# Expert weights loaded by column parts, and exp taken straight from the score PSUM, in a gated cross-attention block with a mixture of experts

## What is computed

```python
# x (8, 100, 512), ctx (8, 722, 512), mask (8, 722) bool, H = 512, one head of D = 32
n = layernorm(x)
q, k, v = n @ Wq + bq, ctx @ Wk + bk, ctx @ Wv + bv
s = q @ k.T / sqrt(512)
s = (s - mean(s)) / (std(s, ddof=1) + 1e-8)            # over the 722 keys
attn = softmax(s + where(mask, -1e-32, 0))
x = x + tanh(g_xattn) * (tile(attn @ v, 16) @ Wout + bout)
n = layernorm(x)
w, idx = top2(softmax(n @ router_w.T)); w = w / (w.sum() + 1e-6)
# 8 experts, w13 (8, 512, 2048), w2 (8, 1024, 512)
y = sum over the two experts of w * ((silu(n @ gate) * (n @ up)) @ w2)
x = x + tanh(g_ffn) * y
```

## Time and profile before

| | us |
|---|---|
| median of 3 runs | 531.41 |
| lowest, highest | 523.58, 532.26 |
| profiled execution, its own time | 529.5 |
| its span in the trace | 527.9 |
| mean granted clock of TensorE in it | 0.858 |

### The profile page before, as it was taken

One profiled execution on the slowest core, in us unless ns is written; L12 is line 12 of the kernel. 1 busy time (PEld: TensorE's weight loads), 2 busy tenths in 40 slices (PEclk: granted clock), 3 DMA queues, 4 the chain that ended last, 5 costly groups with the idle time before them and its releaser, 6 DMA issues.

```text
span 527.9 us, 7587 instructions
## 1 busy us (share of the span) xinstructions
PE 422.1 (80%) x2108; PEld 307.7 (58%) x2109; DVE 243.1 (46%) x491; ACT 195.6 (37%) x319; POOL 194.9 (37%) x340
## 2 busy tenths in 40 slices
PE   3668986888662129999994099999999999999991
PEld 1234554445441127778773078777877877787781
DVE  0245663445545131475571454138537557367220
ACT  0032331232424211473560552237447266265220
POOL 2433475676657421234343003220413434235121
PEclk9796895766755559999998579999999999999997
DMA  7554665449210007626816706901492671880021
GB/s 220 174 185 159 192 201 130 151 152 353 76 34 13 0 21 264 236 40 199 321 34 230 279 0 214 333 23 23 130 368 42 222 291 30 285 265 21 5 40 13
DMA packets 25795, 78.78 MB, mean 149 GB/s; under 512 B 6041, under 2 KB 6049, under 8 KB 20658
## 3 DMA queue, kind: packets, MB, share of 16 engines
q1 hardware_dynamic: 19266, 67.51, 35.4%
q0 software_dynamic: 4752, 7.80, 8.2%
q10 hardware_dynamic: 1760, 3.28, 2.0%
HBM read 71.92 MB, written 7.57 MB: 151 GB/s over the span
## 4 chain that ended last, share of the span: by engine, by line
PE 61%; POOL 11%; DMA 9%; issue 8%; DVE 4%; SPq 2%; ACT 1%; POOLq 1%; DVEq 0%; ACTq 0%
PE scp L476 16%; PE turnA L456 16%; PE turnB L456 15%; PE kvp L463 2%; PE kvp L410 2%; DMA stage<-in_L_ffn_w_dram 2%; PE kvp L332 2%; POOL lists_d L969 2%; DMA ent_next<-lists_d 2%; DMA xg<-xn_d,gidx 2%; PE scp L442 1%; PE turnA L425 1%; POOL hot L998 1%; DMA g_in<-in_g_ffn_dram 1%; POOL rs L921 1%
## 5 line engine op out<-in xcount | busy, mean ns | idle before, releaser
L691 DVE TENSOR_TENSOR w13l<-stage,w13h 128x1024 fp32r<-128x1024 f32 x64 | 76.4, 1219 | 26.2 <-ACT w13h L537 25.8
L537 ACT ACTIVATE w13h<-stage 128x1024 fp32r<-128x1024 f32 x64 | 64.7, 1052 | 22.5 <-DMA stage<-in_L_ffn_w_dram 22.5
L476 PE MATMUL scp<-w2h,hTh 128*128 128x512 f32 x128 | 56.8, 444 | 2.3 <-DVE hTl L862 2.3
L456 PE MATMUL turnA<-w13h,xTh 128*128 128x512 f32 x128 | 53.2, 416 | 4.8 <-DVE xTl L851 4.8
L456 PE MATMUL turnB<-w13h,xTh 128*128 128x512 f32 x128 | 51.9, 406 | 0.0
L476 PE MATMUL scp<-w2l,hTh 128*128 128x512 f32 x128 | 51.6, 403 | 0.0
L456 PE MATMUL turnA<-w13l,xTh 128*128 128x512 f32 x128 | 51.5, 403 | 0.0
L456 PE MATMUL turnA<-w13h,xTl 128*128 128x512 f32 x128 | 51.5, 403 | 0.0
L476 PE MATMUL scp<-w2h,hTl 128*128 128x512 f32 x128 | 51.2, 400 | 0.0
L456 PE MATMUL turnB<-w13h,xTl 128*128 128x512 f32 x128 | 50.6, 395 | 0.0
L456 PE MATMUL turnB<-w13l,xTh 128*128 128x512 f32 x128 | 50.5, 395 | 0.0
(11 more groups left out here) (167 smaller groups left out, 737.2 us busy)
## 6 DMA issues: line engine op xcount, KB each, us to landing
stage<-in_L_ffn_w_dram SPq DMA_DIRECT2D x48, 1024.0 KB, 11.8
ctx_t<-in_ctx_dram SPq DMA_DIRECT2D x8, 1444.0 KB, 7.3
mterm<-mterm_d SPq DMA_DIRECT2D x8, 282.0 KB
x_t<-in_x_dram SPq DMA_DIRECT2D x8, 200.0 KB
out_dram<-x ACTq DMA_DIRECT2D x8, 200.0 KB
xn_d<-xn ACTq DMA_DIRECT2D x8, 200.0 KB
ctx_t<-in_L_xattn_Wout_dram SPq DMA_DIRECT2D x1, 1024.0 KB, 7.1
ent_next<-lists_d POOLq DMA_DIRECT2D x17, 1.0 KB, 2.0
```

What stands on the lines that cost most here:

```text
L456: mm = pe.matmul(region, xp[:, c, :], rhs, start=(c == 0 and i == 0), stop=(c == HC - 1 and i == 2))
L476: mm = pe.matmul(scp[:, 512:512 + H], hp[:, q, j * P:(j + 1) * P], wp[:, q * QC + j, :], start=(q == 0 and j == 0 and i == 0), stop=(q == ...
L537: act.activation(dst, src, ACT.Copy).then_inc(S["w_hi"], 1)
L691: dve.tensor_tensor(lo, raw, hi.bitcast(F32), ALU.subtract).then_inc(S["w_lo"], 1)
```

## The change

Expert weights: the host lays w13 out by column part (8 experts, 4 parts, 128 partitions, 2048 values: one part is 1 MB with 8 KB in a row for each partition) and w2 by halves in the same way. `stage13`, `w13h` and `w13l` have the part as their outer dimension. Part q is loaded when units 2q and 2q + 1 of the expert before are split; there is no wait for a gather except for the first. ACT waits for one part before the two units that read it.

Attention: exp is taken from `scp` in PSUM with scale and bias in one instruction, without z, maximum and accumulated sum. The mask becomes a factor `emask` = exp(term), 128 x 8 x 6, multiplied into the values when these are copied to `vn`. A 65th column of `vn` holds `emask` itself, so that the head has a 65th row with the softmax's sum. The bias row of the output is a 65th row of `wsum`: multiplied by the sum and divided again by it, it comes in with the output. The sum is brought to the partitions of the tokens by a matmul with one column (`pick_sum`), and its reciprocal is taken from there. x is kept in four buffers, so that `xc` is not needed.

```diff
-        mterm_d = nc.dram_tensor("mterm_d", [NB, SK], F32).ap()
-        stage13 = sb(es, "stage13", [P, HC, I2])
+        stage13 = sb(es, "stage13", [P, NQ, HC, 2 * QW])
-        x_t = [sb(a, f"x_t{i}", [SQ, H]) for i in range(2)]
+        x_t = [sb(a, f"x_t{i}", [SQ, H]) for i in range(4)]
-        vn = [sb(a, f"vn{i}", [P, KT, 2 * D]) for i in range(2)]
+        vn = [sb(a, f"vn{i}", [P, KT, 2 * D + 1]) for i in range(2)]
...
             for b in range(1, NB):
-                s = S[f"x_in{b % 2}"]
-                if b >= 2:
-                    sp.wait_ge(S["xn_ready"], b - 1)
-                    sp.wait_ge(S["xc_ready"], b - 1)
-                sp.dma_start(x_t[b % 2][:], x[b]).then_inc(s, 16)
-                load_mterm(b - 1)
+                if b >= 4:
+                    sp.wait_ge(S["x2_ready"], b - 3)
+                elif b == 2:
+                    sp.wait_ge(S["crow_done"], 1)
+                elif b == 3:
+                    sp.wait_ge(S["rw_turned"], 1)
+                sp.dma_start(x_t[b % 4][:], x[b]).then_inc(S[f"x_in{b % 4}"], 16)
...
             sp.wait_ge(S["attn_done"], 4)
+            sp.wait_ge(S["gathered"], 16)
             with sp.Fori(1, E) as e:
-                sp.wait_ge(S["w_lo"], e * W_UNITS - 2)
-                before = sp.value_load(first_tile[0:1, bass.ds(e - 1, 1)], min_val=0, max_val=TILES - 1)
-                sp.wait_ge(S["gathered"], before * 16 + 32)
-                for c in range(HC):
-                    sp.dma_start(stage13[:, c, :], w13[bass.ds(e, 1), c * P:(c + 1) * P, :].rearrange("o p n -> p (o n)")
-                                 ).then_inc(S[f"st13_{c}"], 16)
+                for q in range(NQ):
+                    sp.wait_ge(S["w_lo"], e * W_UNITS - W_UNITS + 2 * q + 2)
+                    sp.dma_start(stage13[:, q, :, :], w13[bass.ds(e, 1), q].rearrange("o p (c n) -> p (o c) n", c=HC)
+                                 ).then_inc(S[f"st13_{q}"], 16)
...
-            def softmax_z(b):
+            def softmax_exp(b):
                 act.wait_ge(S["sig_ready"], b + 1)
                 act.wait_ge(S["scores_done"], b + 1)
                 if b >= 1:
-                    act.wait_ge(S["exp_done"], b)
-                act.activation(z[:], scp[0:SQ, 0:SK], ACT.Identity, bias=sig[:, 5:6], scale=sig[:, 3:4]).then_inc(S["z_done"], 1)
-
-            def softmax_exp(b):
-                act.wait_ge(S["negmax"], b + 1)
-                if b >= 1:
                     act.wait_ge(S["prob_turned"], b)
-                    act.wait_ge(S["gsum"], b)
-                act.activation(prob[:], z[:], ACT.Exp, bias=zmax[:, 1:2], accum_out=psum_p[:]).then_inc(S["exp_done"], 1)
+                act.activation(prob[:], scp[0:SQ, 0:SK], ACT.Exp, bias=sig[:, 5:6], scale=sig[:, 3:4]).then_inc(S["exp_done"], 1)
 
             def split_hi(e, unit, last):
 
-                if unit == 0:
-                    for c in range(HC):
-                        act.wait_ge(S[f"st13_{c}"], e * 16 + 16)
+                if unit < 2 * NQ and unit % 2 == 0:
+                    act.wait_ge(S[f"st13_{unit // 2}"], e * 16 + 16)
...
                     pe.wait_ge(S["head_copied"], b + 1)
+                    if b == 0:
+                        pe.wait_ge(S["pick_made"], 2)
+                    pe.matmul(turnB[0:SQ, 640:641], headT[:], pick_sum[:], start=True, stop=True).then_inc(S["sum_done"], 1)
                     if live(i):
                         pe.wait_ge(S["v_copied"], 2 * (i + 1))
                     pe.matmul(turnA[0:SQ, 0:H], headT[:], wsum[:], start=True, stop=True).then_inc(S["out_done"], 1)
...
-                    dve.tensor_copy(vn[i % 2][:, 0:KT - 1, :], turnA[:, 0:(KT - 1) * 2 * D].rearrange("p (k d) -> p k d", d=2 * D)
-                                    ).then_inc(S["v_copied"], 1)
+                    dve.tensor_tensor(vn[i % 2][:, 0:KT - 1, 0:2 * D],
+                                      turnA[:, 0:(KT - 1) * 2 * D].rearrange("p (k d) -> p k d", d=2 * D),
+                                      emask[:, i, 0:KT - 1].unsqueeze(2).to_broadcast([P, KT - 1, 2 * D]), ALU.mult
+                                      ).then_inc(S["v_copied"], 1)
...
+                    dve.wait_ge(S["sum_done"], b + 1)
+                    if b >= 1:
+                        dve.wait_ge(S["x2_ready"], b)
+                    else:
+                        dve.wait_ge(S["tanh_done"], 1)
+                    dve.reciprocal(gs[:, 0:1], turnB[0:SQ, 640:641]).then_inc(S["sum_inv"], 1)
+                    dve.wait_ge(S["sum_inv"], b + 1)
+                    dve.tensor_scalar(gs[:, 1:2], gs[:, 0:1], g_t[0:SQ, 0:1], None, ALU.mult).then_inc(S["gsum"], 1)
                     dve.wait_ge(S["out_done"], b + 1)
...
             for i in ROUNDS:
+                if live(i):
+                    if i == 0:
+                        pool.wait_ge(S["emask_made"], 1)
+                    if i >= 2:
+                        pool.wait_ge(S["head_done"], i - 1)
+                    pool.tensor_copy(vn[i % 2][:, :, 2 * D:2 * D + 1], emask[:, i, :].unsqueeze(2)).then_inc(S["vsum_set"], 1)
...
-                if live(i + 1) and i >= 0:
-                    residual(i + 1)
```

More of the change, by code:

```diff
@@ L26, in gated_block @@
     D = Wq.shape[1]
-    E, _, I2 = w13.shape
-    I = I2 // 2
+    E, NQ, _, UW = w13.shape
     HC = H // P
+    QW = UW // HC // 2
+    I = NQ * QW
     IC = I // P
@@ L92, in gated_block @@
         qT = sb(a, "qT", [2 * D, SQ])
-        headT = sb(a, "headT", [2 * D, SQ])
-        xc = [sb(a, f"xc{i}", [SQ, H]) for i in range(3)]
+        headT = sb(a, "headT", [2 * D + 1, SQ])
+        pick_sum = sb(a, "pick_sum", [2 * D + 1, 1])
         x2 = [sb(a, f"x2{i}", [SQ, H]) for i in range(2)]
@@ L110, in gated_block @@
         g_t = sb(a, "g_t", [P, 2])
-        crow = sb(a, "crow", [SQ, H])
         tri = sb(a, "tri", [SQ, SQ])
@@ L319, in _ @@
             pe.wait_ge(S["wsum_copied"], 1)
-            pe.wait_ge(S["bv_spread"], 1)
             pe.wait_ge(S["small_in"], 16 * 7)
-            pe.matmul(scp[0:SQ, 0:H], bv_b[:], wsum[0:D, :], start=True, stop=False)
-            pe.matmul(scp[0:SQ, 0:H], ones[0:1, 0:SQ], bout_r, start=False, stop=True).then_inc(S["crow_done"], 1)
+            pe.matmul(scp[2 * D:2 * D + 1, 0:H], bv_c[:], wsum[0:D, :], start=True, stop=False)
+            pe.matmul(scp[2 * D:2 * D + 1, 0:H], ones[0:1, 0:1], bout_r, start=False, stop=True).then_inc(S["crow_done"], 1)
             pe.wait_ge(S["rw_copied"], 1)
@@ L407, in _ @@
                     pe.wait_ge(S["v_copied"], 2 * (b + 1))
+                    pe.wait_ge(S["vsum_set"], b + 1)
                     for k in range(KT):
                         n = P if k < KT - 1 else KL
-                        mm = pe.matmul(kvp[0:2 * D, 0:SQ], vn[b % 2][0:n, k, :], probT[0:n, k, :], start=(k == 0), stop=(k == KT - 1))
+                        mm = pe.matmul(kvp[0:2 * D + 1, 0:SQ], vn[b % 2][0:n, k, :], probT[0:n, k, :], start=(k == 0), stop=(k == KT - 1))
                     mm.then_inc(S["head_done"], 1)
@@ L454, in gate_up @@
                     for i, (xp, wp) in enumerate(terms):
-                        rhs = wp[:, c, :].rearrange("p (g n) -> p g n", g=2)[:, :, q * QW:(q + 1) * QW]
-                        mm = pe.matmul(region, xp[:, c, :], rhs, start=(c == 0 and i == 0), stop=(c == HC - 1 and i == 2))
+                        mm = pe.matmul(region, xp[:, c, :], wp[:, q, c, :], start=(c == 0 and i == 0), stop=(c == HC - 1 and i == 2))
                 mm.then_inc(S["gu_done"], 1)
@@ L697, in _ @@
                     dve.wait_ge(S["crow_done"], 1)
[L698 to L699 removed]
+                    dve.tensor_copy(wsum[2 * D:2 * D + 1, :], scp[2 * D:2 * D + 1, 0:H]).then_inc(S["crow_copied"], 1)
                 if live(i):
```

135 lines of the change are left out of this document (49 added, 86 removed).

## The result

The changed kernel takes 486.82 us (median of 4 runs, 484.31 to 489.53); the kernel before, in the same rounds, 531.84. The ratio is 0.921, 95% interval 0.909 to 0.933. Executions over 1.5% longer than the fastest of the same kernel, at a lower clock, are left out of the ratios, and of the medians of the kernel before that stand at the head of the experiments. The profiled execution has 484.31 us and a span of 482.7. First the page, then the windows of tiles 3 and 4, which answer to the earlier trace rows.

A forecast was written before the change was run, and what follows sets the result against it. TensorE, busy for 80% of the span, was taken as the bound, with waits in tile 4 and the attention rounds. 529.5 − 21.4 (loads) − 7.2 (attention) = 500.9 us, range 491 to 512.

The forecast's parts named there:

- The loads: Expert stage, tile 4: weight parts loaded as their places come free shorten it from 41.56 to 20.1 us, saving 21.4.
- The fetch of tile 1: Expert stage: list fetch beside expert 1's weight loads makes the gather land 4.6 us later, covered by 7 us, cost nothing.
- Rivals A and D: A (0.02): loads starve the gathers, 540 us. D (0.07): ScalarE still waits in tile 4, 509.9 us.
- The chain terms of attention: Attention rounds: work removed from ScalarE, VectorE and POOL, less the added matmul, sums to −7.2 us by the head's start.
- the last round's −1.9: Attention, head at 147.73: exp straight from PSUM lets the weight splits begin earlier, −1.9 us.
- B: Attention stage gives nothing back, TensorE being next in line in nearly every round; 510.8 us, chance 0.14.
- under 0.5 in most rounds: Attention, sign of being right: head matmul L410 follows the scores directly in most rounds, with waits under 0.5 us.
- over 1 us was to be a sign: Attention, sign of being wrong: head matmul L410 still waits for probT by over 1 us.
- These waits are ceilings: Attention: POOL or VectorE savings count only up to TensorE's head waits of 0.61, 3.87, 1.48 and 1.53 us.
- Rival C: Attention: shorter waits keep the granted clock up, three rounds lose up to 2 us more each; 494.9 us, chance 0.14.
- 13.5 us of POOL's chain as a floor: Attention rounds: the clock gain shortens rounds only as far as POOL's chain of 13.5 us lets them.
- the case of more time at the half level: Attention: the reverse of the higher clock, TensorE spends more time at half clock; 507 us, chance 0.10.

The follow-up runs named there:

- loads_only: The kernel before with its old attention, given the new weight layout, the new loads and the wait by part; 509.91 us, ratio 0.9615.
- after_again: The changed kernel timed once more, nothing altered, as yardstick for the run with the moved instruction; 488.79 us, ratio 0.9195 against the kernel before.
- before_norm: The kernel before with one VectorE instruction, the next batch's normalised x, moved behind the copy of the head; 519.79 us, ratio 0.980.

## Why the prediction was wrong

*The loads: right.* The term was 21.4 us. `loads_only` measured 21.2. In the changed kernel tile 4 is 20.12 us against a forecast of 20.1, with VectorE next in line and TensorE waiting 1.1 us for hTl (forecast 1 to 2). Which half of the edit earns it I had not asked; it is the early start. The fetch of tile 1 grew as the earlier trace rows said and was covered. Rivals A and D are out.

*The chain terms of attention: about right.* First head: −1.85 forecast, −2.2 and −0.9 in two profiles of the changed kernel. From the first head to the eighth the sum has −5.8, which is −7.7 without the 0.3 or 0.4 for the new matmul (the last round's −1.9 leaves it out, against the sum's own rule); idle time changed by −6.0 and −6.4. POOL's place takes 0.18 to 0.37 (forecast 0.2 to 0.4). The output's matmul starts 0.20 us behind the new one at the full level (forecast 0.3), 0.36 at half. With the 65th row of `wsum` it takes 1.08 us at the full level, 1.10 before. The factor on the values takes 0.48 and 0.27 us for its two instructions, where the copies took 0.48 and 0.21. B is out. A miss beside it: the heads of 59.87 and 124.21 still waited 0.61 and 2.28 us, where I had looked for under 0.5 in most rounds; over 1 us was to be a sign that the forecast is wrong.

*The step that failed* is the sentence "These waits are ceilings: what is saved on POOL or VectorE in a round is paid out only up to the wait." It takes TensorE's own work as fixed. 87.0 us of the rounds were busy time at a mean clock of 0.72, and that is no fixed work: it fell by 15.3 us in the first profile of the changed kernel and by 10.9 in the second, 2 to 3% of the span of 527.9. Even the round from the first head to the second, for which I wrote +0.3, lost 4.0 (14.30 to 10.31 us). Its first row before, for the twelve matmuls that answer to the row of 37.88 above:

```profile
40.13 2.26 PE L410 MATMUL kvp<-probT,vn 128*64 128x100 f32 x12
```

2.26 us at a clock of 0.50, 1.25 at 1.00.

*Rival C had the mechanism and not the size.* It gave three rounds up to 2 us each; a fallen round cost 3.9 in `after_again`, and five of the seven rounds stood between 0.61 and 0.70 before. It also took 13.5 us of POOL's chain as a floor, and the rounds of 74.14 and 101.31 took 12.99 and 12.46 us. After the fact, with 15.3 in place of C's 6.0, its 494.9 becomes 485.6; with the second profile's 10.9, it is 490.0. The measured 486.82 and 488.79 lie between. The chance of 0.14 was too low as well, since every attention edit shortened a wait, while the case of more time at the half level had nothing in the trace for it.

## What to carry to other kernels

Split the length of a stage into idle and busy time of the engine that bounds it, and look at the clock column before you call its busy time work. Where TensorE ran small matmuls between waits, a wait cost its length here and perhaps a fallen round behind it (3.9 us in `after_again`), so price both. And look first for an instruction that waits in front of one that doesn't need it: moving a single such instruction gave 4.8 to 10 us here, where all the attention edits together gave 21 to 23.

## What the runs showed of the hardware

- Useless matmuls in front of waits made the kernel before some 8 us faster (`before_fill`, 523.33 us, ratio 0.987) and did nothing for the changed one (`after_fill`, 491.04 against 486.82 and 488.79), in which rounds at 0.62 and 0.63 stayed.
- In `after_again` a round of 95 small matmuls at a clock of 1.00 (13.14 us) is idle for 2.9 us, one with the same matmuls at a mean of 0.60 (17.04) for 0.9. The slower TensorE had less to wait for, so idle time alone understates the other engines' chains.
- The clock of a round isn't a property of the kernel: two executions of the changed kernel had the round from about 75 us at 1.00 and at 0.60. One such round is 3.9 us; the ten runs of the kernel lie within 5.3.
- POOL's conversion of 128 indices took 2.29 us beside VectorE's subtraction with two SBUF inputs (274.27 us, kernel before) and 0.23 without it (265.92 us, `before_norm`); in the kernel before the expert's loads waited behind it.
- The list fetch of tile 1 waited 5.36 us beside weight loads (changed kernel, mean DMA share 0.98 from 171.31 to 177.27 us) where it waited 1.71 alone (kernel before, share 0.01 from 194.88 to 197.18 us).
